# Row maxima of both halves by one VectorE instruction, over two banks taken from the ring of the score pairs, under a new written-out order

## The reference

```python
for l in range(4):                       # cut to what matters
    x = layernorm(x + attn_l(x))         # L0a, heads1, L2a, self3
    x = layernorm(x + xattn_l(x, ctx))   # L0x, L1x, L2x, L3x
    x = layernorm(x + ffn_l(x))          # ffn0, moe1, ffn2, moe3
# in L0a, L2a and the four xattn:  softmax(q k^T * scale + mask) v, by 16 heads of 8
```

## Time and profile before

| | us |
|---|---|
| median of 3 runs | 1750.06 |
| the 3 runs | 1750.02, 1750.06, 1759.99 |
| the profiled execution's own time | 1757.96 |
| its span, first to last instruction | 1756.2 |
| PE, DVE, ACT, POOL busy | 1378.9, 1085.2, 738.3, 369.8 |
| mean granted TensorE clock | 0.866 of full |

### The profile page before, as it was taken

One profiled execution on the slowest core, in us unless ns is written; L12 is line 12 of the kernel. 1 busy time (PEld: TensorE's weight loads), 2 busy tenths in 40 slices (PEclk: granted clock), 3 DMA queues, 4 the chain that ended last, 5 costly groups with the idle time before them and its releaser, 6 DMA issues.

```text
span 1756.2 us, 25812 instructions
## 1 busy us (share of the span) xinstructions
PE 1378.9 (79%) x9530; PEld 656.8 (37%) x9530; DVE 1085.2 (62%) x2336; ACT 738.3 (42%) x1036; POOL 369.8 (21%) x475
## 2 busy tenths in 40 slices
PE   3568887785665686687577987988998999978986
PEld 1234332331331351343133544543344444434443
DVE  3648866778569579578766646756234524256766
ACT  1055654644323213214345542346644545532652
POOL 3034432006105206304432012022211100020000
PEclk8579988886567796798698989999999999988999
DMA  7421232100100310330222124131211321023011
GB/s 169 113 56 33 55 52 42 34 1 26 36 0 2 72 37 2 85 75 4 57 47 59 38 55 83 33 96 27 62 36 37 82 52 61 2 58 64 25 37 60
DMA packets 50072, 86.35 MB, mean 49 GB/s; under 512 B 13718, under 2 KB 42198, under 8 KB 45526
## 3 DMA queue, kind: packets, MB, share of 16 engines
q1 hardware_dynamic: 49950, 84.71, 21.0%
HBM read 66.95 MB, written 15.60 MB: 47 GB/s over the span
## 4 chain that ended last, share of the span: by engine, by line
PE 46%; DVE 18%; DMA 11%; POOL 7%; SPq 7%; issue 6%; ACT 5%; POOLq 0%; ACTq 0%; DVEq 0%
PE ps L897 5%; PE ps L1051 5%; PE ps L824 5%; DMA KH<-scratch 5%; DVE MX L1261 5%; PE ps L1017 4%; SPq L2025 4%; PE ps L1018 4%; PE ps L1024 3%; POOL SIDE L1937 3%; PE ps L830 3%; DMA scratch<-HQ 2%; PE ps L858 2%; PE ps L735 2%; ACT WORK L1683 2%
## 5 line engine op out<-in xcount | busy, mean ns | idle before, releaser
L1261 DVE TENSOR_REDUCE MX<-ps 128x3 f32<-128x462 f32 (+5 forms) x704 | 411.7, 626 | 233.4 <-PE ps L830 170.2
L1683 ACT ACTIVATE WORK<-ps 128x1024 f32<-128x1024 f32 (+1 forms) x352 | 319.7, 945 | 204.0 <-PE ps L858 123.9
L824 PE MATMUL ps<-KH,QH 48*128 48x154 bf16 (+5 forms) x1536 | 147.1, 279 | 178.0 <-DVE MX L1261 66.1
L824 PEld LDWEIGHTS ps<-KH,QH 48*128 48x128 bf16 (+1 forms) x1536 | 61.9, 99 | 334.7 <-DVE MX L1261 151.7
L897 PE MATMUL ps<-WORK,VA 128*18 128x512 f32 (+3 forms) x1536 | 171.4, 535 | 10.3 <-POOL WORK L1923 6.4
L1937 POOL TENSOR_TENSOR SIDE<-SIDE 128x512 f32<-128x512 f32 x64 | 113.1, 1799 | 269.1 <-ACT SIDE L1752 228.2
L1923 POOL TENSOR_SCALAR_AFFINE_SELECT WORK<-WORK 128x256 f32<-128x256 f32 (+1 forms) x192 | 93.8, 495 | 355.6 <-ACT WORK L1683 354.8
L1777 ACT ACTIVATE SIDE<-ps 128x512 f32<-128x512 f32 x96 | 57.3, 597 | 253.9 <-PE ps L1018 253.6
L858 PE MATMUL ps<-QH,KH 54*128 54x512 bf16 (+3 forms) x768 | 120.2, 359 | 13.8 <-ACT WORK L1683 10.8
L1507 DVE TENSOR_TENSOR SIDE<-SIDE,ps 128x512 f32<-128x512 f32 x96 | 65.6, 686 | 98.0 <-ACT SIDE L1777 97.5
L1024 PE MATMUL ps<-SIDE 128*128 128x128 f32 x768 | 111.0, 292 | 15.3 <-DVE SIDE L1507 13.0
(11 more groups left out here) (279 smaller groups left out, 2194.9 us busy)
## 6 DMA issues: line engine op xcount, KB each, us to landing
SIDE<-in_experts SPq DMA_DIRECT2D x96, 192.0 KB, 2.4
scratch<-HQ SPq DMA_DIRECT2D x48, 192.0 KB, 3.0
QH<-scratch SPq DMA_DIRECT2D x48, 192.0 KB
...
```

The source lines that it names most:

```text
L824: mms[b] = pe.matmul(banks[b][:, c * pitch:c * pitch + width], qr[b][:, h, t * 128:t * 128 + 128], kr[b][:, h, 0:width], start=(c == 0), s ...
L1261: dve.tensor_reduce(MX[:, 32 * b + i0:32 * b + i0 + cnt], src, AX.X, ALU.max, negate=True).then_inc(freed, 1)
L1683: act.activation(PB[:, N % NSLOT, :, lo:hi], wide_banks("pair", F, n)[:, :, lo:hi], ACT.Exp).then_inc(sem("exp_done"), 1)
```

## The change

`max` leaves the narrow ring and joins the wide one: a step takes two adjacent banks there. One VectorE instruction reduces both banks and writes the maxima of both halves. There are 352 such instructions where there were 704. The narrow ring keeps its three banks for the other kinds. TensorE's instructions are the same in number and shape; it signals once for a step, after the last matmul. The tables of the order are others: `FRONT_ORDER`, `SIDE_ORDER`, `TAIL_ORDER` and the whole of `STEPS`, of which the diff shows the first two lines.

```diff
--- before.py
+++ after.py
@@ -141,9 +141,9 @@
 CHAIN = ["L0a", "L0x", "ffn0", "heads1", "L1x", "moe1", "L2a", "L2x", "ffn2", "self3", "L3x", "moe3"]
 ATTENTION = {L.name: li for li, L in enumerate(LAYERS)}
 EXPERTS = {"moe1": NE, "moe3": NE3}
-NARROW = ("project", "max", "turn", "out", "mix", "wo", "mean", "q0x", "q0t", "h0t", "h0b", "qkv", "ht", "log", "rank", "w0", "w3",
+NARROW = ("project", "turn", "out", "mix", "wo", "mean", "q0x", "q0t", "h0t", "h0b", "qkv", "ht", "log", "rank", "w0", "w3",
           "base", "rest", "dn", "acc", "hid2", "f3", "fk3", "pt3", "fin")
-WIDEK = ("pair", "h0", "gu", "g2", "s3")
+WIDEK = ("max", "pair", "h0", "gu", "g2", "s3")
 RELEASE = {"ffn0": "wo", "heads1": "ht", "moe1": "acc", "ffn2": "wo", "self3": "wo", "moe3": "acc"}
 
 
@@ -242,90 +242,88 @@
 
 FIRST = {"ffn0": ("q0x", 0), "heads1": ("qkv", 0), "moe1": ("log", 0), "moe3": ("log", 0), "ffn2": ("wide", 0), "self3": ("f3", 0)}
 FRONT_ORDER = """
-L0a.0 L0a.1 L0a.2 L0a.3 L0x.0 L0x.1 L0x.2 L0x.3 L1x.0 L1x.1 L2a.0 L1x.2 L2a.1 L1x.3 L2x.0 L2x.1 L2a.2 L2a.3 L2x.2 L2x.3
-L3x.0 L3x.1 L3x.2 L3x.3
+L0a.0 L0a.1 L0a.2 L0a.3 L0x.0 L0x.1 L0x.2 L0x.3 L1x.0 L1x.1 L1x.2 L2a.0 L1x.3 L2a.1 L2x.0 L2a.2 L2x.1 L2a.3 L3x.0 L2x.2
+L2x.3 L3x.1 L3x.2 L3x.3
 """.split()
 SIDE_ORDER = """
-ffn0.0 ffn0.1 heads1.0 ffn0.2 ffn0.3 heads1.1 moe1.0 heads1.2 moe1.1 heads1.3 moe1.2 moe1.3 ffn2.0 ffn2.1 self3.0
-self3.1 ffn2.2 ffn2.3 self3.2 self3.3 moe3.0 moe3.1 moe3.2 moe3.3
+ffn0.0 ffn0.1 ffn0.2 ffn0.3 heads1.0 heads1.1 heads1.2 moe1.0 heads1.3 moe1.1 moe1.2 moe1.3 ffn2.0 self3.0 ffn2.1
+self3.1 moe3.0 ffn2.2 ffn2.3 self3.2 self3.3 moe3.1 moe3.2 moe3.3
 """.split()
 TAIL_ORDER = """
-L0a.0 L0a.1 L0a.2 L0a.3 L0x.0 L0x.1 ffn0.0 L0x.2 ffn0.1 L0x.3 heads1.0 ffn0.2 ffn0.3 L1x.0 heads1.1 moe1.0 L1x.1
-heads1.2 moe1.1 heads1.3 L2a.0 L1x.2 L2a.1 moe1.2 L1x.3 L2x.0 moe1.3 L2x.1 L2a.2 ffn2.0 L2a.3 ffn2.1 self3.0 self3.1
-L2x.2 L2x.3 ffn2.2 L3x.0 ffn2.3 self3.2 self3.3 L3x.1 moe3.0 L3x.2 moe3.1 L3x.3 moe3.2 moe3.3
+L0a.0 L0a.1 L0a.2 L0a.3 L0x.0 L0x.1 ffn0.0 L0x.2 L0x.3 ffn0.1 ffn0.2 ffn0.3 heads1.0 heads1.1 L1x.0 heads1.2 L1x.1
+moe1.0 L1x.2 heads1.3 moe1.1 L2a.0 L1x.3 moe1.2 L2a.1 L2x.0 moe1.3 ffn2.0 self3.0 L2a.2 L2x.1 L2a.3 ffn2.1 self3.1 L3x.0
+L2x.2 L2x.3 moe3.0 L3x.1 ffn2.2 ffn2.3 self3.2 self3.3 moe3.1 L3x.2 L3x.3 moe3.2 moe3.3
 """.split()
 STEPS = """
-project*5 base pieces project send project*4 max*5 pieces max*9 send max*8 split project*2 max turn max project max pair
-max project pair max pair max pair*2 max pair project value*3 pieces rest max pair*2 max pair max pair max value pair
...
+project*5 base pieces project*3 send project max*4 project max*11 pieces max*6 send max split project max*2 turn max*2
+project max pair project max project pair max*3 project max*2 value pieces pair max*2 pair*2 max*4 pair value pair max
...
@@ -349,8 +347,6 @@
         kind, _, times = step.partition("*")
         for _ in range(int(times or 1)):
             out.append(waiting[kind].pop(0))
-            if kind == "max":
-                out.append((kind, out[-1][1], out[-1][2] + 1))
     assert not any(waiting.values()), waiting
     return out
 
@@ -805,7 +801,8 @@
                 cnt = units[0][2]
                 rows = ROW_M if L.mask == "keys" else ROW_MASK
                 qr, kr = ([f(F, b, rows) for b in range(2)] for f in (QROWS, KROWS))
-                banks = [ring("max", F, u), ring("max", F, u + 1)]
+                pairs = wide("max", F, u)
+                banks = [pairs[:, b, :] for b in range(2)]
                 width = KC if L.cross else 128 * (units[0][1] // HH + 1)
                 pitch = KP if L.cross else width
                 masks = []
@@ -829,8 +826,7 @@
                             lhsT, rhs = mask_parts(b, mask, at, n)[part]
                             mms[b] = pe.matmul(banks[b][:, o:o + n], lhsT, rhs, start=False, stop=(part == 1),
                                                skip_group_check=True)
-                for b in range(2):
-                    mms[b].then_inc(ring_filled, 1)
+                mms[1].then_inc(all_wide, 1)
 
             def turn_maxima(F):
 
@@ -1109,7 +1105,7 @@
                     rest_setup()
                 elif kind == "project":
                     project(key, i)
-                elif kind == "max" and i % 2 == 0:
+                elif kind == "max":
                     max_units_of(key, i)
                 elif kind == "turn":
                     turn_maxima(key)
@@ -1251,18 +1247,16 @@
 
             def max_unit(F, u):
                 L = layer_of(F)
-                b, i0, cnt = max_units(L)[u]
-                bank = ring("max", F, u)
-                if L.cross:
-                    src = bank[:, 0:cnt * KP].rearrange("p (c k) -> p c k", k=KP)[:, :, 0:KC]
-                else:
-                    w = 128 * (i0 // HH + 1)
-                    src = bank[:, 0:cnt * w].rearrange("p (c k) -> p c k", k=w)
-                dve.tensor_reduce(MX[:, 32 * b + i0:32 * b + i0 + cnt], src, AX.X, ALU.max, negate=True).then_inc(freed, 1)
+                _, i0, cnt = max_units(L)[u]
+                wide_filled(dve, "max", F, u)
+                pitch, width = (KP, KC) if L.cross else (128 * (i0 // HH + 1),) * 2
+                src = wide_banks("max", F, u)[:, :, 0:cnt * pitch].rearrange("p b (c k) -> p b c k", k=pitch)[:, :, :, 0:width]
+                dst = MX[:].rearrange("p (b i) -> p b i", b=2)[:, :, i0:i0 + cnt]
+                dve.tensor_reduce(dst, src, AX.X, ALU.max, negate=True).then_inc(wide_freed, 1)
 
             def split_maxima(F):
 
-                consumed(dve, "max", F, len(max_units(layer_of(F))) - 1)
+                wide_consumed(dve, "max", F, len(max_units(layer_of(F))) - 2)
 
                 def piece(i):
                     return MP[:, :, :, i, :].rearrange("p t b h -> p b t h")
```

More of the change, by code:

```diff
@@ new lines @@
+pair copy max project pair*2 value pair value max pair project pair max turn max pair value pair max*3 value pair*2
+max*2 value max pair out pair max value max pair value pair max value max copy max project max*2 pieces max*3 pair value
+pair*2 split value send pair*2 value*3 rest pair max*2 out pair value pair max mix pair max value max pair wo pair max
+square value max copy pair value pair max pair value pair*2 turn out max pair value pair*2 mean pair max value x value
+max pair value max pair value*2 max copy pair value pair max project pair*2 project out project pair value pair project
@@ new lines @@
+pair max value pair max value pair max pair pieces value*2 pair max mix max send pair wo pair max value*2 square max
+copy pair mean max pair value x split pair*2 value pair turn pair value pair masks project pair value pair max project
+out pair*2 value*2 pair value*2 copy pair*2 value pair*2 value pair*2 value pair w0 out pair*2 value max*2 project*2
+value pieces pair max mix send pair max wo tables2 pair max value*3 square pair copy max mean max pair x value max*2 out
+pair max pair value pair split pair value pair value max*2 turn project pair max value max value pair project max
@@ new lines @@
+pair*2 acc pair max log max pair wo max pair value max pair square value top ew pair*2 mean max x gu project pair
+value*3 pair rank project pair*2 project pair*2 value*3 max pair project pair ew*2 max dn gu*2 ew project dn copy ew
+pieces max dn gu pair value max split dn pair*2 value ew value pair gu*2 send turn out pair dn pair dn pair max*2 value
+max pair value pair max value pair max value*2 copy ew max pair out ew max*2 value pair max*2 pair*2 max mix max*2 wo
+max square max value max gu*2 value pair max copy dn*2 max value max*2 mean max*2 value ew pair*2 split out x ew turn gu
@@ new lines @@
+project*2 max*2 dn max ew dn max gu project*2 pieces max*2 dn gu max*2 dn ew send max split gu ew gu ew turn max dn
+max*2 ew dn gu*2 pair dn max dn pair*2 value pair max pair acc pair*2 value max pair value pair max copy wo pair max
+value max*2 value max value split square copy out*2 turn mix mean wo square x pair mean pair x value pair*2 log ew top
+ew pair*2 value*2 copy pair ew gu*2 value pair*2 dn*2 pair gu ew value gu dn value dn copy out ew out ew gu*2 mix dn wo
+dn ew*2 square gu*2 mean dn*2 x acc log ew*2 top gu*2 ew dn ew dn gu fin gu dn*2 ew*2 wo gu*2 ew dn ew dn gu*2 square
@@ L329 @@
+dn*2 mean acc wo square x mean fin x fin
 """.split()
```

115 lines of the change are left out of this document (46 added, 69 removed).

## The result

The changed kernel takes 1742.07 us (median of 15 runs, 1735.84 to 1749.01); the kernel before, on the same chip, 1753.24 us (15 runs). The ratio is 0.9936 with a 95% interval of 0.9916 to 0.9955, that is 11 us faster (8 to 15). The prediction was 23 us faster: the sign holds, the size is half. The profiled execution has a span of 1740.6 us, against 1756.2.

What follows compares the result with a forecast made beforehand. TensorE, busy 1378.9 of 1756.2 us, was taken as the bound, with VectorE nearly so from 80 to 900 us. Terms -9 - 10 - 30 + 18 + 8 + 0 = -23 us gave a 1727 us median, range 1698 to 1773.

Steps and rivals of the forecast that it cites:

- Part 1: All 352 maxima steps: one fused reduction saves 0.06 us a step, 21 us less VectorE work; 128x1024 takes 1.225 us.
- Part 2: First 22 maxima steps, from 48 us on: two slots cut a step from 1.67 to about 1.25 us, 9 us gained.
- Part 3: The other 330 maxima steps: 20 us less VectorE work, half counted as time, 10 us gained.
- Part 4: TensorE's waits for operands from DRAM at fronts' first maxima: the new order covers more of them, 30 us gained.
- The prediction's own signs of being wrong: Forecast wrong if waits for operands don't fall, or if ffn2.2 to self3.3 loses over 40 us.
- Part 5: Places the covering work leaves: 18 us lost between ffn2.2 and self3.3, 8 us at ffn0.2, ffn0.3 and heads1.0.
- Part 6: Maxima and pairs taking turns in two wide slots: 0 taken, between 47 us gained and 46 lost.
- rival B: Expert units, maxima alternating with `gu`: the shared ring stalls TensorE by 46 us, giving 1773 us; chance 0.18.
- A: First maxima: waits only move, as two slots without other work take what covering operand waits gives; 1742 us; chance 0.28.

Runs made afterwards that it cites:

- experiment 3: Changed kernel with its one reduction over two banks written as two, one a bank; 1758.56 us, ratio 1.0032 to the kernel before.
- experiments 6 and 8: On the changed kernel: old steps under heads1, 1745.63 us; L3x.2's first maxima later, 1742.88; L3x.1's end inside ffn2.2 and ffn2.3, 1738.15; both latter moves, 1737.83.
- experiment 2: Changed kernel, fused reduction and shared wide ring kept, with the order tables of the kernel before; 1844.90 us, ratio 1.0533 to the kernel before.
- Experiment 5: Changed kernel with steps and tails up to the end of ffn0.3 in the old order, then the new; 1768.91 us, ratio 1.0118 to the kernel before.

## Why the prediction was right in its sign and wrong in its size

**Part 1, the fused instruction's duration: right.** 1.220 us measured for 128x1024 where 1.225 was forecast, 1.114 for 128x924 where it was 1.12. VectorE fell by 21.4 us for the instruction itself (experiment 3), 0.061 us a step where 0.06 was forecast. One side remark was wrong: in a row of maxima the saving was to be up to 0.105 us a step, and it is 0.05 over the 22 steps of the start. The Trainium skill (VectorE: DVE Perf Modes, the section on the TRN2 errata) gives 120 cycles besides the elements; by an estimate from that, 0.125 us for each instruction saved. The traces do not agree with it, and the measurement decides.

**Part 2, the dense start: right**, and a little better: 11.0 us for the 22 steps where 9 were forecast, by the mechanism given. The layer norm of L0a.3 ends 9.0 us earlier (289.3 against 298.3).

**Part 3, the other steps: probably too small.** Half of 20 us was counted, 10; the later 264 steps alone brought 14.9, give or take 4, and the instruction in all 16.8 of its 21.4 us. The reason for the half was that TensorE is busy 86 to 93% in the later stretches. But a maximum is still what the next pair or maximum waits for, by its slot. With two reductions TensorE waits for maxima so:

```profile
PE ps L821 <- DVE MX L1256: 32.6, 68, 2.1
...
PE ps L854 <- DVE MX L1256: 16.6, 28, 6.8
```

With one it waits 26.6 and 12.7 us, which is 9.9 of the 16.8 us.

**Part 4, the waits for operands: the step that failed.** The order did what was forecast: 100.3 us became 65.5. It was counted as 30 us of time, and no run shows any of it. Rings and order with two reductions came to +5.6 us (1 to 10); the forecast for them was part 2's 9, less about 1 of the instruction, part 4's 30 against 18 and 8 of part 5, so -12. The two differ by 18 us, more than the 11 to 12 us by which the whole forecast is off, because part 3 made up for some of it. Where single waits were taken out (experiments 6 and 8: 43.2, 9.35 and, in all but a third, 6.47 us), at most 3.4 us followed. Only the 9.35 us were a wait for keys, so that part 4's waits are no time is shown for one of them and argued for the others. In these three places TensorE stood while something else, VectorE's work, a layer norm or a transfer, set the pace; with the wait gone, it stood elsewhere or did its work at the lower clock. The prediction's own signs of being wrong, that these waits don't fall or that ffn2.2 to self3.3 loses over 40 us, did not come up: they looked at idle time, too.

**Part 5, the bare units: forecast in idle time, which at heads1 was no time.** From L2a.3 to self3.3 there are 13 us more idle, where 18 were forecast. At ffn0 and heads1 it was 46 more instead of 8, because the forecast counted the work that leaves, 15 us, and not the VectorE chain of heads1 that is then alone on the path. But covering heads1 gained nothing. Covering a part of ffn2 gained 3.4 us in the profiled execution and nothing that the medians can tell; what the whole bare stretch there costs is open. So parts 4 and 5 both counted idle time as time. That they nearly cancel (-30 and +26) is luck, and kept the forecast from being further off.

**Part 6, the shared ring: mis-sized.** 0 was taken. The waits for maxima and exponentials in the rings are 62.6 us now. Before, they were 66.1 and 10.8, of which 19 belong to part 2: 58. So 5 us more. Waits that the kernel before hardly has add some 9: maxima wait 4.9 us for an expert's product, and `gu` 4.3 for maxima and 1.5 for exponentials, where only pairs waited for a product before, 1.9 us. Under the old order the ring's waits grow by 61 us (experiment 2), more than the 46 of rival B. Its place was wrong: not `gu` above all, but pairs and maxima wait for each other.

Of the rivals, A (the waits only move, 8 us faster) is nearest to the result in mechanism. That its size fits, too, is in part luck: it is added up from 10 us of part 3 and 15 of part 4, and measured were 16.8 us for the instruction and nothing to be seen of part 4. That it was given 0.28 and the forecast 0.48 was the error in weighing. What is not settled is how parts 4, 5 and 6 share what is left: +5.6 us where the dense start alone brought -10.1, so some 16 us lost where the forecast had 4 gained. Experiment 5 and the ring's waits say that the shared ring has a part of it. An estimate by the steps shows how leads open and close. Each kind of step gets TensorE's busy time for it on the changed kernel's page, and both traces are read at the same amount of work done, between ends of layer norms:

```
share of TensorE's work done    24%   34%   53%   82%   90%   100%
changed less before, us         -33   +37    -8   -42   -27    -15
```

TensorE's work done early is a lead. The lead of 33 us turns into a lag of 37 in bare ffn0 and heads1, where VectorE's work comes alone, and by 82% there is a lead of 42. From there on 27 us are lost again, 15 of them up to self3.3, which is near part 5's 18. The estimate weighs TensorE's work alone, so it is no proof; it says why a reading of single waits could not add up.
